# The record stage's table of places kept as two exact 16-bit parts, made on VectorE

## What is computed

```python
edge_index = jnp.stack([src, dst])
x = layernorm(x + net0(x, edge_index, ...))                  # 4 layers: segment_sum(x[src], dst), two products, batch norms
x = layernorm(x + net1(x, edge_index, edge_attr_64, ...))    # segment_sum over src of x[dst] @ W_T + edge_attr_64 @ T
x = layernorm(x + net2(x, edge_attr_16, ..., edge_index))    # ea = silu(edge_attr @ We); 4 layers of relu(x[src] + ea)
x = layernorm(x + net3(x, edge_attr_128, ..., edge_index))   # attention: K[src] * Q[dst] * (edge_attr @ WE)
```

## Time and profile before

| | us |
|---|---|
| median of 3 runs | 10701.52 |
| lowest and highest run | 10679.4 and 10709.26 |
| profiled execution, its own time | 10682.69 |
| its span | 10681.0 |

### The profile page before, as it was taken

The page is one execution under the profiler, slowest core; times in us unless marked ns, Lnnn a source line. Parts: engine busy times, 40 slices in busy tenths (PEclk is TensorE's granted clock), DMA queues, the critical chain, the costliest instruction groups (busy, mean ns, idle before and its releaser), DMA issues.

```text
span 10681.0 us, 246329 instructions
## 1 busy us (share of the span) xinstructions
PE 7847.9 (73%) x65479; PEld 6767.7 (63%) x65480; DVE 7303.3 (68%) x17259; ACT 3898.0 (36%) x7935; POOL 4320.5 (40%) x4160
## 2 busy tenths in 40 slices
PE   4689884667777776865489887787777777597775
PEld 3466663556676676765368676676676666586664
DVE  7476663345755755756656568878778778648998
ACT  0122121320520611602450263553553543575665
POOL 0677674556035044063005306316226136006664
PEclk7555555789899898988699999999899999799997
DMA  8666668466485584673189679689689589398885
GB/s 337 179 196 192 189 189 113 157 235 174 175 290 159 206 267 131 262 242 99 47 248 421 251 291 329 230 304 328 222 309 330 218 312 329 134 385 255 249 247 160
DMA packets 1666229, 2508.24 MB, mean 235 GB/s; under 512 B 406323, under 2 KB 930348, under 8 KB 1665680
## 3 DMA queue, kind: packets, MB, share of 16 engines
q1 hardware_dynamic: 1230926, 1418.34, 40.2%
q0 software_dynamic: 305856, 1048.98, 28.3%
q10 hardware_dynamic: 129282, 39.02, 1.6%
HBM read 1485.24 MB, written 1091.81 MB: 241 GB/s over the span
## 4 chain that ended last, share of the span: by engine, by line
PE 24%; issue 10%; DVE 10%; ACT 2%; SPq 2%; DVEq 1%; DMA 1%; ACTq 0%; POOL 0%; another core or an unknown queue 0%; POOLq 0%
PE ps L949 8%; PE ps L977 6%; PE ps L974 4%; PE ps L944 3%; SPq L691 2%; DVE heads L1800 1%; DVE gath L1812 1%; DVE gath L1795 1%; DVE gath L1733 1%; DVE weights L1781 1%; ACT gath L1262 1%; ACT gath L1220 1%; DVE big L1790 0%; ACT big L1394 0%; DVEq L541 0%
## 5 line engine op out<-in xcount | busy, mean ns | idle before, releaser
L805 POOL DMA_INDIRECT gath<-msg_units,unit_at_d x2176 | 2154.6, 990 | 3606.5 <-DMA msg_units<-gath 2387.8
L977 PE MATMUL ps<-onehot,gath 128*128 128x125 f32 x17408 | 2500.2, 299 | 980.8 <-issue 412.2
L977 PEld LDWEIGHTS ps<-onehot,gath 128*128 128x128 f32 x17408 | 2258.6, 208 | 1222.4 <-issue 936.9
L949 PE MATMUL ps<-big,onehot 125*128 x29376 | 2017.3, 227 | 395.0 <-ACT gath L1220 213.4
L949 PEld LDWEIGHTS ps<-big,onehot 125*128 125x128 bf16 x29376 | 1871.6, 99 | 541.6 <-issue 483.3
L1668 DVE TENSOR_SCALAR onehot<-row_b,part 125x512 bf16<-125x512 uint8 x2720 | 1267.8, 483 | 1076.5 <-PE ps L949 620.5
L1220 ACT ACTIVATE gath<-ps 128x512 f32<-128x512 f32 x2448 | 1417.3, 597 | 1000.4 <-PE ps L949 654.9
L1726 DVE TENSOR_TENSOR onehot<-ps,node_d 128x500 f32<-128x500 f32 x2176 | 1462.7, 673 | 185.3 <-issue 161.7
L1745 DVE TENSOR_TENSOR big<-big,ps 128x125 f32 x2176 | 609.3, 280 | 775.6 <-PE ps L977 718.4
L779 POOL DMA_INDIRECT rec<-big,idx_ring x832 | 966.1, 1161 | 417.4 <-issue 342.4
L1262 ACT ACTIVATE gath<-gath 128x512 f32<-128x512 f32 x1088 | 685.2, 630 | 1104.4 <-issue 558.6
(11 more groups left out here) (264 smaller groups left out, 10459.8 us busy)
## 6 DMA issues: line engine op xcount, KB each, us to landing
msg_units<-gath SPq DMA_DIRECT2D x2176, 256.0 KB
big<-ea_units SPq DMA_DIRECT2D x1088, 256.0 KB
kv_units<-gath SPq DMA_DIRECT2D x272, 512.0 KB
ea_units<-rec SPq DMA_DIRECT2D x16, 4352.0 KB
rec<-gath SPq DMA_DIRECT2D x272, 256.0 KB
big<-rec SPq DMA_DIRECT2D x272, 256.0 KB
big<-in_attr_t SPq DMA_DIRECT2D x208, 256.0 KB
rec<-big SPq DMA_DIRECT2D x1, 43296.0 KB, 152.1
```

Source lines behind the costliest of these rows:

```text
L805: pool.indirect_dma_start(att_slot(q) if way == "attr" else gath[:, q, :], None, units, bass.IndirectOffsetOnAxis(ap=unit_at[w][:, g:g + 1 ...
L949: ins = pe.matmul(ps[:, r, c], hots_t[0:NT, r, c], upper[0:NT, ds(at_[q] + b, D)], start=b == NA * NODES_PAD, stop=b == LOW)
L977: ins = pe.matmul(ps[:, RING + r, 0:NT], unit_ring[:, q, j, :], hots[:, r, j, :], start=j == 0, stop=j == UNIT - 1)
```

## The change

The lookup becomes one of 16-bit products. `tab` is kept as two bfloat16 parts, high and low, of every entry. The high part is the entry rounded to 16 bits, the low part the exact rest. So that both are exact, the start value is shifted by -MIDDLE (line 1490), and the index adds MIDDLE back (line 1613). The turned one-hot is written as bfloat16. Line 884's four float32 products become eight 16-bit ones, two for each column of 128 edges, summed in PSUM. The copy of `run` leaves ACT: `keep_table` and its waits are gone, and DVE makes both parts from PSUM (`table_halves`, two instructions with a wait for `run_ready`), between the ranks of group g and its wait for `look_ready`. The setup makes the offset table's two parts with five instructions where it had two.

```diff
--- before.py
+++ after.py
@@ -53,6 +53,8 @@
 TRIPS = -(-GROUPS // (2 * Q)) * 2
 GROUPS = TRIPS * Q
 UNITS = GROUPS * P
+MIDDLE = 2 * UNITS
+assert MIDDLE < 2 ** 17
 SLOTS = UNITS * UNIT
 SURE = E // GSLOTS
 GCOLS = -(-GROUPS // P)
@@ -333,8 +335,9 @@
         lower = earlier[:, (PER - 1) * P:]
         before = part_of_big([P, P])
         ones = part_of_big([P, P])
-        tab = part_of_big([BKT, 2, 2 * BKT])
+        tab = part_of_big([BKT, 4 * BKT]).bitcast(BF16).rearrange("p (r h b) -> p r h b", r=2, h=2)
         turned_e = part_of_big([BKT, 2, PER * P])
+        turned_h = turned_e[:, 0, :].bitcast(BF16).rearrange("p (r e) -> p r e", r=2)
         tile_b = part_of_big([BKT, RING, PER * P // 4]).bitcast(U8)
         key_b = part_of_big([P, RING, PER * P // 2]).bitcast(U16)
 
@@ -880,9 +883,9 @@
                         pe.wait_ge(turned, g + 1)
                         if not (first and q < 2):
                             pe.wait_ge(looked, g - 1)
-                        for k in range(PER):
-                            last = pe.matmul(ps[:, 3 * r, k * 2 * BKT:(k + 1) * 2 * BKT], turned_e[:, r, k * P:(k + 1) * P],
-                                             tab[:, r, :], start=True, stop=True)
+                        for k, h in ((k, h) for k in range(PER) for h in range(2)):
+                            last = pe.matmul(ps[:, 3 * r, k * 2 * BKT:(k + 1) * 2 * BKT], turned_h[:, r, k * P:(k + 1) * P],
+                                             tab[:, r, h, :], start=h == 0, stop=h == 1)
                         last.then_inc(look_ready, 1)
 
                         pe.wait_ge(att_in[q], 16 * (1 + PER) * (i + 1))
@@ -1145,12 +1148,6 @@
                        .then_inc(keys_out[b % 2], 16)
 
             def scatter(n):
-                def keep_table(g, q, first):
-                    act.wait_ge(run_ready, g + 1)
-                    if not first:
-                        act.wait_ge(look_ready, g - 1)
-                    act.activation(tab[:, q % 2, 0:BKT], ps[0:BKT, 2, 0:BKT], ACT.Copy).then_inc(tab_kept, 1)
-
                 def load_a64(g, q, trip):
                     if trip is not None:
                         act.wait_ge(rec_out[q], 16 * PER * trip)
@@ -1172,15 +1169,12 @@
                 def trip(i, head, last):
                     for q in range(RING):
                         g = RING * i + q
-                        if not (last and q == RING - 1):
-                            keep_table(g + 1, (q + 1) % RING, head == 0 and q == 0)
                         load_a64(g, q, None if head == 0 else i)
 
                         if q:
                             evict(g - 1, q - 1)
                         elif head != 0:
                             evict(g - 1, RING - 1)
-                keep_table(0, 0, True)
                 trip(0, 0, False)
                 trip(1, 1, False)
                 with act.Fori(2, LOADS - 1) as i:
@@ -1487,7 +1481,7 @@
                 ch.link(dve.tensor_scalar(start_of[:, :], ps[0:BKT, 5, 0:2], float(P), None, ALU.mult))
                 for w in range(2):
                     ch.link(dve.tensor_scalar(base_u[:, w, :], pre[:, w, :], start_of[:, w:w + 1], None, ALU.add))
-                dve.tensor_scalar(quad[:, :], base_u[:, 0, :], float(UNIT), None, ALU.mult).then_inc(table_step, 1)
+                dve.tensor_scalar(quad[:, :], base_u[:, 0, :], float(UNIT), float(-MIDDLE), ALU.mult, ALU.add).then_inc(table_step, 1)
 
                 ch.link(dve.tensor_copy(starts_row[:, :, :], ps[:, 4, 0:128].rearrange("p (w b) -> p w b", b=64)[:, :, 0:BKT]))
                 for c in range(GCOLS):
@@ -1509,9 +1503,15 @@
                 ch.link(dve.tensor_tensor(blank_f[:, :], blank_f[:, :], some[:, :], ALU.mult))
                 ch.mark(dve.tensor_scalar(blank_at[:, :], blank_f[:, :], tr, None, ALU.add))
                 dve.wait_ge(table_sums, 3)
+                ch.wait()
+                ch.link(dve.tensor_tensor(blank_f[:, :], ps[0:BKT, 6, 0:BKT], base_u[:, 0, :], ALU.subtract))
                 for k in range(2):
-                    last = dve.tensor_tensor(tab[:, k, BKT:2 * BKT], ps[0:BKT, 6, 0:BKT], base_u[:, 0, :], ALU.subtract)
-                ch.link(last)
+                    ch.mark(dve.tensor_copy(tab[:, k, 0, BKT:2 * BKT], blank_f[:, :]))
+                ch.wait()
+                for k in range(2):
+                    ch.mark(dve.tensor_tensor(tab[:, k, 1, BKT:2 * BKT], blank_f[:, :], tab[:, k, 0, BKT:2 * BKT],
+                                              ALU.subtract))
+                ch.wait()
                 dve.wait_ge(vals_in, 16)
                 dve.tensor_copy(meta_e[:, :, 0], src_v).then_inc(stage_done, 1)
 
@@ -1579,11 +1579,19 @@
                     dve.wait_ge(tile_in[q], 16 * (trip + 1))
                     if not fresh:
                         dve.wait_ge(look_ready, g - 1)
-                    dve.tensor_scalar(turned_e[:, q % 2, :], tile_b[:, q, :], part[0:BKT, 0:1], None, ALU.is_equal)\
+                    dve.tensor_scalar(turned_h[:, q % 2, :], tile_b[:, q, :], part[0:BKT, 0:1], None, ALU.is_equal)\
                        .then_inc(turned, 1)
 
+                def table_halves(g, q):
+                    dve.wait_ge(run_ready, g + 1)
+                    ch.link(dve.tensor_copy(tab[:, q % 2, 0, 0:BKT], ps[0:BKT, 2, 0:BKT]))
+                    dve.tensor_tensor(tab[:, q % 2, 1, 0:BKT], ps[0:BKT, 2, 0:BKT], tab[:, q % 2, 0, 0:BKT], ALU.subtract)\
+                       .then_inc(tab_kept, 1)
+
+                table_halves(0, 0)
+
                 def lap(i, first, last_lap):
-                    ch.trip(i, 4 * RING)
+                    ch.trip(i, 5 * RING)
                     for q in range(RING):
                         g = i * RING + q
                         if first and q == 0:
@@ -1600,6 +1608,7 @@
                                                             bucket[:, ds(g * PER + k, 1)], earlier[:, (PER - 1 - k) * P:],
                                                             ALU.is_equal, ALU.mult, accum_out=rank_e[:, k:k + 1])
                         last.then_inc(ranked, 1)
+                        table_halves(g + 1, q + 1)
                         dve.wait_ge(look_ready, g + 1)
                         dve.tensor_tensor(prod, ps[:, 3 * (q % 2), 0:PER * 2 * BKT].rearrange("p (k t b) -> p k t b", k=PER, t=2),
                                           oh_e[:, q, 1, :, :].unsqueeze(2).to_broadcast([P, PER, 2, BKT]), ALU.mult)\
@@ -1610,13 +1619,13 @@
                         dve.wait_ge(ranked, g + 1)
                         if not first:
                             dve.wait_ge(rec_out[q], 16 * PER * i)
-                        ch.link(dve.tensor_tensor(idx_ring[:, q, :], look[:, :, 0], rank_e[:, :], ALU.add))
+                        ch.link(dve.scalar_tensor_tensor(idx_ring[:, q, :], look[:, :, 0], float(MIDDLE), rank_e[:, :], ALU.add, ALU.add))
                         ch.link(dve.tensor_single_scalar(unit_i[:, :], idx_ring[:, q, :], 2, ALU.arith_shift_right))
                         ch.mark(dve.tensor_tensor(rec_r[:, q, :, AT_META + 3].bitcast(I32), unit_i[:, :], look[:, :, 1], ALU.add))
                         ch.wait()
                         dve.nop(nofuse=True).then_inc(placed, 1)
                 laps(dve, LOADS, lap)
-                ch.leave(LOADS, 4 * RING)
+                ch.leave(LOADS, 5 * RING)
 
             def metadata(n):
                 for b in (REST, LOW):
```

## The result

The changed kernel is slower by about 30 us. Median of 12 runs each: 10727.05 us (10718.64 to 10742.07) against 10696.52 us before (10679.40 to 10716.86); the ratio is 1.003, 95% interval [1.0022, 1.0038]. The forecast was 10634, range 10560 to 10705. Two later series on other chips gave much the same: 10721.83 against 10688.09 (1.0033 [1.0021, 1.0045]) and 10628.07 against 10601.91 (1.0026 [1.0015, 1.0036]).

What follows compares the result with a forecast made beforehand. Bound: POOL (5.95 us a group) and PE (5.78), waiting for each other within the record stage's 6.52. Profiled 10682.7, -60 for half the ceiling, +1 setup, +10 from profiled execution to median: 10634, range 10560 to 10705.

Steps and rivals of the forecast that it cites:

- The lookup: Line 884's products in the record stage: from 2.00 to 0.9 us a group, saving PE 1.1, as slack only.
- the ceiling's share: Record stage: half of the 119 us that POOL never waiting would save is gained, taken as -60 us.
- The late signals: Record stage: PE's signals reach ACT and DVE about 6 us late in part of the groups, reason unknown.
- Rival C: Record stage: signals stay late until POOL idles, so the loss returns through `rec_mm`; 0 to -20 us, 10683; chance 0.24.
- The halves on VectorE: Two DVE instructions, about 0.46 us a group: its step goes from 4.98 to 5.44, hidden under POOL's 5.95.
- My price without the cover: Cost of DVE's two added instructions in the record stage if not hidden: 0.46 x 208 = 96 us.
- The gate: DVE's new wait for `run_ready` ahead of `look_ready`: ends before the old wait and costs nothing if signals come in order.
- rival D's loop: Run, late signal, two halves on DVE, next run: 6.9 us a group, stage +79 us, 10772; chance 0.10.
- POOL's stretch: DVE's new instructions lengthening POOL's in the record stage: taken as nothing, with 20 us kept for the range.
- The forecast's ceiling: Record stage with POOL never waiting: 208 x 5.95 = 1237 us, 119 less than 1356, POOL's instructions untouched.
- The variant of B with slow products: Rival of all POOL's waits going (10575, chance 0.22): PE's real work is longer than modelled, so cutting returns over 1.1 us.
- Setup: Offset table made with five instructions instead of two ahead of the blanks' release: +1 us on the path.

Runs made afterwards that it cites:

- act_split: The changed kernel with the table's two 16-bit parts made on ACT instead of DVE; against the kernel before 0.9991 (late signals), 0.9999 and 1.0000 (prompt signals).
- move_copy: The kernel before with only the float32 table copy moved from ACT to DVE: 0.9990, 0.9992, 0.9994 with prompt signals; not run with late signals.
- pool_rest: The kernel before with a rest of about 2 us for POOL ahead of each lap of four groups: +32 us with late signals, +104 with prompt ones.
- dve_extra: The kernel before with two unused 51 x 51 instructions added on DVE in every group, no new wait: +34 us with late signals, -30 with prompt ones.
- act_extra: The kernel before with two unused 51 x 512 instructions (Abs and Relu) added on ACT: 1.0001 with prompt signals; not run with late signals.
- turn_on_act: The changed kernel with the turned one-hot made on ACT instead of DVE: 0.9848, -150 us against the kernel before, with prompt signals; not run with late ones.
- no_loads: The kernel before with edge-feature loads made in the first lap only (wrong output): -59 us with late signals, +17 with prompt ones.

## Why the prediction was wrong

**The lookup.** Forecast 0.9 us a group, measured 0.83; PE's work fell by 1.04 us a group (1203 - 987 = 216 us). Right. That this slack gives a gain was wrong: act_split shows 0 to 19 us for it (net of ACT's added work), where I took 60. The failed step is the ceiling's share: "I take half of the ceiling". I read 5.78 and 5.95 against 6.52 us as two engines that hinder each other near their bounds. They don't: on chips with prompt signals move_copy, with the float32 lookup and PE at the same work, runs at POOL's 5.90. On the chips of the forecast the stage stays above it where signals are late, and relieving PE did not take them away: act_split_third has 806 us of waits that end with "remote", the changed kernel on the same chip 953.

**The late signals.** Rival C comes nearest to what the waits did: the loss returned through `rec_mm`. Its condition, that signals stay late until POOL idles, is not shown. ACT's wait for the counting products is gone, and its wait for `rec_mm` is now 527 us of "remote", where the kernel before, whose ACT waited for the counting products first, had 8:

```profile
L1165 ACT ACTIVATE big<-ps 128x512 f32<-128x512 f32 x205 | 122.0, 595 | 188.3 <-DMA rec<-big,idx_ring 93.8 <-issue 80.3 <-remote 8.3
```

In the changed kernel's trace 260 signals of PE between 400 and 1700 us are recorded more than 1 us after the work's end, and 205 of them arrive in POOL's gaps of over 0.4 us, which together last 247 us of the stage's 1396. In the trace of before it is 146 of 282, in 153 us. That speaks for C, but a gap lasts until the signals come, so they must fall into it whatever holds them. And others arrive while POOL is making descriptors: 98 of the 282 before, and 143 of 236 in act_split_third. pool_rest agrees in part: 72 of 104 us come back. I gave C 0.24, and a time of 10683; the halves' cost came on top.

**The halves on VectorE.** Their size was right: 199 and 206 ns, and a step of 5.46 us where I had 5.44. That they are hidden was wrong, and this is the step that turned the sign: "so it becomes 5.44, under POOL's 5.95: hidden, with 0.5 us to spare". It compares two steps that run without waits. VectorE doesn't: a late signal stops it for some 4 us once or twice a lap, as at 755.60, and what counts, as I read it, is how fast it makes that up. In groups where POOL doesn't wait, POOL takes 5.97 us a group before (mean of 153) and 5.76 after (mean of 139), so VectorE gained 5.97 - 4.98 = 1.0 us a group on POOL before and 0.3 after, and POOL finds `placed` late: 103 us. dve_extra, which adds only this work, gives +34 us, though there most of POOL's waits end with `rec_ready`; that the work costs is shown by experiment, the way by which it does is argued. My price without the cover was 96 us; a third of it was paid.

**The gate.** I said that the new wait would end before the old one and cost nothing. It idles only 33.6 us, so rival D's loop (its first half collecting most of the delay) didn't happen; the sign was D's, its mechanism wasn't. PE does wait 232 us for the second half, but PE isn't the bound. A cost of the gate itself is not needed to account for the loss; it wasn't measured alone where signals are late.

**The sum.** With late signals, act_split (the lookup, with ACT's added work) is worth -10 us and VectorE's work +34, together +24, against +26 to +34 measured. The two come from different chips, and the first has an interval of 19 us, so the agreement is rough.

**POOL's stretch.** I kept 20 us for VectorE's new instructions stretching POOL. POOL's mean fell, from 1161 to 1102 ns: the instructions of over 1.9 us went from 107 to 27, all of them beside the ranks. The Trainium skill ("SBUF — State Buffer", "Who interferes with whom") expected no stretch from the halves, and the traces agree: 1168 ns in dve_extra with such halves, 1166 in act_split and 1175 in act_extra without, on the same chip. By the same section VectorE's 51 x 512 comparison, with one SBUF input, would stretch POOL only in a 2-port mode, and the trace agrees that it doesn't by itself (0.96 us beside it alone), though moving it took 172 ns off POOL's mean. The forecast's ceiling took POOL's lengths as given; turn_on_act's stage of 1082 us lies under its 1237.

**The variant of B with slow products** finds no support: a PE that really ran longer would have returned more than 1.1 us a group when its products were cut, and act_split returned 10 us in all.

**Setup.** The records began at 356.1 us against 353.2, but at 353.6 and 349.2 in the two other profiles of the changed kernel: the +1 us is below what these show.

## What to carry to other kernels

Work that is moved to an engine with slack in its unstalled step isn't free when that engine is stopped now and then by something outside: ask how fast it makes up a stop against the engine that it feeds, before and after. When an engine sits under its bound and the trace ends its waits with "remote", relieving the neighbour that seems late may bring nothing; find first what the lateness follows, and don't take a signal that arrives in a gap for one that the gap let out. To say which instruction stretches another, look at which ones overlap the long cases, not only at what an edit removed. And time a change on more than one chip where the trace has such waits: here one edit, with the change, was worth -150 us on one kind and, in the kernel before, +144 on the other.

## What the runs showed of the hardware

- The kernel before takes 10004 to 10009 us on two chips and 10602 to 10697 on others. In the trace of before 282 of TensorE's signals in the record stage are recorded over 1 us late, at a median of 4.1 us (longest 12.7); in move_copy's trace, from a faster chip, none is, and in ten traces from faster chips not one wait ends with "remote". Why some chips do this is open.
- Late signals can come out together (ACT and DVE released 0.1 us apart at 755.60). Of the changed kernel's 260, 205 arrive in POOL's gaps; of act_split_third's 236, 143 arrive while POOL is making descriptors. With fewer loads (no_loads) and with a rest for POOL (pool_rest) the waits that end with "remote" are 600 and 662 us, against 953 in the changed kernel on the same chip; before has no trace there.
- POOL's indirect DMA of 128 records takes 0.96 us and a gap of 0.3. Beside VectorE's ranks (three operands, 128 x 128 to 128 x 512) it can take up to 1.98: all 298 of over 1.1 us in the trace of before overlap them. Beside VectorE's 51 x 512 comparison alone (uint8 in) it isn't stretched (77 of 0.96 us), yet with that comparison on ACT only 81 of turn_on_act's 832 are over 1.1 us.
- On these data no version was found that beats both kernels on both kinds of chip: act_split is level with before (0.9991 and 1.0000) and 36 us faster than the change.
